# Eight-batch cross attention and non-local block: the first batch's keys and values in context chunks, the second half's rows kept whole, and new engine orders

## Time and profile before

| | us |
|---|---|
| median of 3 runs (lowest, highest) | 1065.98 (1063.28, 1066.46) |
| the profiled execution | 1065.61 |
| its span, first to last instruction | 1063.8 |
| TensorE busy in it | 1042.0 |
| VectorE busy | 722.1 |
| ScalarE busy | 480.6 |
| GpSimd busy | 280.5 |

### The profile page before, as it was taken

How to read it: one execution, slowest core, us unless ns; L and a number is a source line. 1 busy time by engine, 2 the same in 40 slices (tenths; PEclk the granted TensorE clock), 3 DMA queues, 4 the chain that set the end, 5 groups by cost and what they waited for, 6 DMA issues and landing times.

```text
span 1063.8 us, 13869 instructions
## 1 busy us (share of the span) xinstructions
PE 1042.0 (98%) x5104; PEld 850.5 (80%) x5104; DVE 722.1 (68%) x961; ACT 480.6 (45%) x810; POOL 280.5 (26%) x199
## 2 busy tenths in 40 slices
...
DMA packets 80627, 122.06 MB, mean 115 GB/s; under 512 B 13104, under 2 KB 46384, under 8 KB 80560
## 3 DMA queue, kind: packets, MB, share of 16 engines
...
## 4 chain that ended last, share of the span: by engine, by line
PE 88%; DVE 6%; DMA 3%; ACT 1%; issue 1%; SPq 0%; DVEq 0%; ACTq 0%
PE pG L573 33%; PE pG L472 13%; PE pG L584 8%; PE pG L480 6%; PE pG L513 4%; PE pG L487 4%; PE pT L594 3%; PE pS L525 3%; PE pT L525 2%; PE pG L594 2%; PE pM L552 2%; PE pM L561 2%; PE pS L451 2%; PE pT L462 2%; DVE xr L902 2%; DMA out_dram<-xr 1%
## 5 line engine op out<-in xcount | busy, mean ns | idle before, releaser
L573 PE MATMUL pG<-pt,vT 128*128 128x512 f32 x1536 | 352.9, 389 | 1.0 <-DVE pt L852 1.0
L573 PEld LDWEIGHTS pG<-pt,vT 128*128 128x128 f32 x1536 | 287.2, 188 | 60.2 <-issue 1.2
L472 PE MATMUL pG<-wv,x2s 128*128 128x512 f32 x768 | 182.9, 393 | 0.5 <-DVE vT L799 0.4
L881 DVE SCALAR_TENSOR_TENSOR xr<-pG,cl,xr 128x512 f32<-128x512 f32 x64 | 48.0, 751 | 189.2 <-PE pG L573 179.9
L931 POOL TENSOR_TENSOR xms<-xr,xms 128x512 fp32r<-128x512 f32 x64 | 87.7, 1370 | 319.6 <-ACT xms L726 319.6
L472 PEld LDWEIGHTS pG<-wv,x2s 128*128 128x128 f32 x768 | 142.1, 188 | 33.3 <-issue 3.3
L726 ACT ACTIVATE xms<-xr 128x512 fp32r<-128x512 f32 x64 | 40.3, 629 | 203.9 <-DVE xr L881 203.9
L852 DVE TENSOR_TENSOR pt<-mv,pt 128x512 fp32r<-128x512 f32 x128 | 89.8, 753 | 35.6 <-ACT pt L703 35.6
L923 POOL TENSOR_TENSOR x2Ts<-x2T_f,x2Ts 128x512 fp32r<-128x512 f32 x64 | 90.5, 1452 | 72.8 <-ACT x2Ts L672 72.7
L927 POOL TENSOR_TENSOR ys<-yf,ys 128x256 fp32r<-128x256 f32 x32 | 27.3, 854 | 306.1 <-ACT ys L694 306.1
L584 PE MATMUL pG<-xms,wth 128*128 128x512 f32 x384 | 90.1, 391 | 0.0
...
## 6 DMA issues: line engine op xcount, KB each, us to landing
mv<-tp SPq DMA_DIRECT2D x512, 64.0 KB, 2.0
...
```

The costliest lines, as they stand in the source:

```text
L472: last = mm(bank, x2s[:, l, c, 128 * m:128 * m + 128], wv[:, r, c, :], start=(c == 0 and n == 0), stop=(c == 3 and n == 2))
L573: last = mm(bank, vT[:, l, m, 128 * c:128 * c + 128], pt(h)[:, r, m, :], start=(m == 0 and n == 0), stop=(m == 7 and n == 2))
```

## The change

Three things are edited, and the orders are written anew.

1. In batch 0, `k:0 k:1 v:0 v:1` and `v:2 v:3` become `kv:0` to `kv:3`: for each context chunk as it lands, its share of `k` and of four value tiles. They accumulate in six banks at once, `pS`, `pG` and `pM` (`v_bank`). The `wv` chunks are loaded between the context chunks.
2. In half 1, ScalarE adds the constant to the row buffer in place (`xc:c`, after the low part was made), `wy:1,c` adds the product to that and is stored from there; `out:1,c` is gone. In half 0, `wy` and `out` write to `oh`, in the place of the low part, and have a semaphore of their own for the stores (`s_so`), so that `wy:1,c` no longer waits for the store of half 0.
3. ScalarE's `x2T` waits for the last `th` product and no longer for `out:1,c`. Its `k` and `q` wait for stores of half 0.

The lists `FIRST` and `LATER` change for TensorE, ScalarE and VectorE, the same words otherwise, and in particular `x2:2`, `x2:3`, `xs:1` and `x1:1` of the next batch go behind `th:1,1` on ScalarE, and `gs` behind `v:2` on TensorE. GpSimd's lists stay.

```diff
 FIRST = dict(
     pe=(
-        "k:0 k:1 v:0 v:1 q:0 q:1 v:2 v:3 S:0 S:1 v:4 S:2 L:0 L:1 L:2 S:3 L:3 gs S:4 G:0 G:1 gt G:2 G:3 v:5 S:5 "
...
+        "kv:0 kv:1 kv:2 kv:3 q:0 q:1 v:4 S:0 S:1 L:0 L:1 L:2 S:2 S:3 gs L:3 G:0 S:4 gt G:1 G:2 GT:0 G:3 GT:1 v:5 "
+        "S:5 S:6 v:6 v:7 Y:0 S:7 Y:1 Y:2 Y:3 PV:0,0,0 M:0 M:1 PV:0,0,1 PV:0,1,0 PV:0,1,1 PV:0,2,0 B:0 B:1 "
...
     act=(
...
+        "w:0 x2:0 w:1 w:2 x2:1 xs:0 x2:2 w:3 xs:1 x2:3 w:4 xs:2 x1:0 w:5 x1:1 xs:3 x1:2 x1:3 k s v:0 k2 x2T:0 q "
+        "v:1 x2T:1 v:2 x2T:2 x2T:3 q2 x2T:4 v:3 v:4 x2T:5 x2T:6 x2T:7 w:6 S:0 L:0 w:7 S:1 L:1 L:2 gs S:2 L:3 S:3 "
+        "gt G:0 G:1 S:4 T:0 G:2 GT:0 G:3 w:8 GT:1 T:1 v:5 v:6 S:5 v:7 T:2 Y:0 T:3 Y:1 Y:2 Y:3 S:6 S:7 mts T:4 "
...
 LATER = dict(
     pe=(
-        "gs k:0 k:1 q:0 q:1 v:0 v:1 v:2 S:0 S:1 gt L:0 L:1 S:2 L:2 S:3 L:3 G:0 S:4 G:1 GT:0 G:2 G:3 v:3 S:5 v:4 "
-        "v:5 v:6 GT:1 v:7 Y:0 S:6 S:7 Y:1 Y:2 Y:3 PV:0,0,0 M:0 M:1 PV:0,0,1 PV:0,1,0 PV:0,1,1 B:0 B:1 PV:0,2,0 "
+        "k:0 k:1 q:0 q:1 v:0 v:1 v:2 gs S:0 S:1 L:0 L:1 L:2 gt S:2 S:3 L:3 G:0 G:1 G:2 GT:0 GT:1 G:3 S:4 S:5 v:3 "
+        "v:4 v:5 v:6 v:7 Y:0 S:6 S:7 Y:1 Y:2 Y:3 PV:0,0,0 M:0 M:1 PV:0,0,1 PV:0,1,0 B:0 B:1 PV:0,2,0 PV:0,1,1 "
...
     act=(
-        "xs:2 xs:3 s x1:2 x1:3 k x2T:0 x2T:1 x2T:2 q x2T:3 x2T:4 x2T:5 v:0 x2T:6 q2 v:1 k2 x2T:7 gs v:2 gt S:0 "
-        "L:0 L:1 S:1 L:2 S:2 L:3 S:3 G:0 GT:0 G:1 T:0 S:4 v:3 T:1 G:2 G:3 v:4 v:5 T:2 GT:1 v:6 S:5 v:7 T:3 Y:0 "
-        "Y:1 Y:2 Y:3 S:6 S:7 mts PV:0,0 PV:0,1 T:4 T:5 T:6 B:0 B:1 T:7 PV:0,2 PV:0,3 PV:1,0 PV:1,1 PV:1,2 +x2:0 "
-        "PV:1,3 +x2:1 th:0,0 +xs:0 +x2:2 th:0,1 +x1:0 +x2:3 th:1,0 +x1:1 +xs:1 th:1,1"
+        "x2:2 xs:1 x2:3 xs:2 x1:1 x1:2 x1:3 xs:3 x2T:0 x2T:1 x2T:2 q s k x2T:3 v:0 x2T:4 x2T:5 q2 x2T:6 k2 v:1 "
+        "v:2 gs x2T:7 S:0 L:0 S:1 gt L:1 L:2 S:2 L:3 S:3 G:0 GT:0 T:0 G:1 G:2 v:3 GT:1 G:3 S:4 T:1 v:4 v:5 S:5 "
+        "v:6 T:2 v:7 Y:0 T:3 Y:1 Y:2 Y:3 S:6 mts S:7 PV:0,0 T:4 T:5 T:6 PV:0,1 PV:0,2 T:7 PV:0,3 PV:1,0 PV:1,1 "
+        "B:0 PV:1,2 xc:0 B:1 +x2:0 xc:1 xc:2 th:0,0 PV:1,3 +x2:1 xc:3 th:0,1 +x1:0 th:1,0 +xs:0 th:1,1"
     ),
     dve=(
-        "k q v:0 q2 k2 v:1 v:2 S:0 S:1 n:0 tr:0 S:2 n:1 tr:1 S:3 n:2 tr:2 G:0 S:4 G:1 n:3 G:2 tr:3 G:3 T:0 G2:0 "
-        "G2:1 v:3 T:1 G2:2 G2:3 GT:0 v:4 S:5 v:5 n:4 tr:4 GT:1 v:6 n:5 v:7 Y:0 tr:5 T:2 Y:1 T:3 Y:2 Y:3 S:6 S:7 "
-        "n:6 tr:6 mt n:7 mts tr:7 PV:0,0 PV:0,1 T:4 T:5 T:6 PV:0,2 B:0 T:7 B:1 PV:0,3 PV:1,0 PV:1,1 PV:1,2 PV:1,3 "
-        "+x2:0 +x2:1 th:0,0 +x2:2 th:0,1 +x2:3 th:1,0 th:1,1 wy:0,0 wy:0,1 out:0,0 wy:0,2 +s wy:0,3 out:0,1 "
-        "wy:1,0 out:0,2 out:0,3 wy:1,1 out:1,0 out:1,1 wy:1,2 wy:1,3 out:1,2 out:1,3"
+        "s q v:0 k q2 k2 v:1 v:2 S:0 S:1 n:0 tr:0 n:1 S:2 tr:1 S:3 n:2 G:0 tr:2 G:1 G:2 n:3 G2:0 tr:3 G:3 S:4 "
+        "GT:0 S:5 T:0 v:3 G2:1 n:4 G2:2 GT:1 v:4 tr:4 v:5 T:1 G2:3 n:5 v:6 v:7 T:2 Y:0 tr:5 Y:1 T:3 Y:2 S:6 Y:3 "
+        "n:6 tr:6 S:7 mt mts n:7 PV:0,0 tr:7 T:4 PV:0,1 T:5 PV:0,2 T:6 T:7 PV:0,3 PV:1,0 PV:1,1 PV:1,2 B:0 PV:1,3 "
+        "B:1 +x2:0 th:0,0 +x2:1 th:0,1 th:1,0 th:1,1 +x2:2 wy:0,0 out:0 wy:0,1 +x2:3 out:1 wy:0,2 wy:0,3 out:2 "
+        "out:3 wy:1,0 wy:1,1 wy:1,2 wy:1,3"
     ),
...
+        oh = [at(f"oh{c}", [128, 512], F, rd + 4096 * c + 2048) for c in range(4)]
...
+        def v_bank(b, m):
+            if b == 0 and m in (2, 3):
+                return pM[:, m - 2, :]
+            return bank_of(use_v(b, m))
...
+                        dst = out[b, 128 * c:128 * c + 128, 512 * h:512 * h + 512]
+                        if h:
+                            wait_free(eng, b, G_WY + 4 + c)
+                            eng.dma_start(dst, xr[c][:, :]).then_inc(s_st[c], 16)
+                        else:
+                            wait(eng, "oa", b, c)
+                            eng.dma_start(dst, oh[c][:, :]).then_inc(s_so[c], 16)
...
+            def do_kv(b, c):
+                if c == 0:
+                    eng.wait_ge(s_wlo, W_K + 1)
+
+                def k_mm(part):
+                    for h in range(2):
+                        last = mm(pS[:, h, :], wk[:, c, :], x2s[:, part, c, 512 * h:512 * h + 512],
+                                  start=(c == 0 and part == HI), stop=(c == 3 and part == LO))
+                        if c == 3 and part == LO:
+                            done(last, "k")
+
+                def v_mm(m, n):
+                    l, r = PASSES[n]
+                    return mm(v_bank(0, m), x2s[:, l, c, 128 * m:128 * m + 128], wv[:, r, c, :],
+                              start=(c == 0 and n == 0), stop=(c == 3 and n == 1))
+
+                wait(eng, "x2hi", 0, c)
+                k_mm(HI)
+                eng.wait_ge(s_whi, W_V + 1 + c)
+                if c < 3:
+                    for m in range(4):
+                        v_mm(m, 0)
+                    wait(eng, "x2lo", 0, c)
+                    k_mm(LO)
+                    for m in range(4):
+                        v_mm(m, 2)
+                    eng.wait_ge(s_wlo, W_V + 1 + c)
+                    for m in range(4):
+                        v_mm(m, 1)
+                else:
+                    wait(eng, "x2lo", 0, c)
+                    k_mm(LO)
+                    eng.wait_ge(s_wlo, W_V + 1 + c)
+                    for m in range(4):
+                        v_mm(m, 0)
+                        v_mm(m, 2)
+                        done(v_mm(m, 1), "g")
+
...
             def do_x2T(b, m):
                 eng.wait_ge(s_x2Td[m // 2], 16 * (b + 1))
                 if b:
-                    wait(eng, "oa", b - 1, 4 + m // 2)
+                    wait(eng, "g", b - 1, G_TH + 3)
...
+            def do_xc(b, c):
+                wait(eng, "xlo", b, 4 + c)
+                if b == 0:
+                    eng.wait_ge(s_cst, 4)
+                done(act(xr[c][:, :], xr[c][:, :], ACT.Identity, bias=cst(c)), "xc")
...
             def do_wy(b, h, c):
                 i = G_WY + 4 * h + c
                 wait(eng, "g", b, i)
-                if h == 0:
-                    wait(eng, "xlo", b, 4 + c)
+                if h:
+                    wait(eng, "xc", b, c)
+                    done(stt(out=xr[c][:, :], in0=bank_of(i), scalar=gain(c), in1=xr[c][:, :],
+                             op0=ALU.mult, op1=ALU.add), "gf")
                 else:
-                    eng.wait_ge(s_st[c], 16 * (2 * b + 1))
-                done(stt(out=xr[c][:, :], in0=bank_of(i), scalar=gain(c), in1=xms(h)[:, c, LO, :].bitcast(F),
-                         op0=ALU.mult, op1=ALU.add), "gf")
-
-            def do_out(b, h, c):
-                wait_free(eng, b, G_WY + 4 * h + c)
-                done(stt(out=xr[c][:, :], in0=xr[c][:, :], scalar=cst(c), in1=xms(h)[:, c, HI, :].bitcast(F),
+                    done(stt(out=oh[c][:, :], in0=bank_of(i), scalar=gain(c), in1=xms0[:, c, LO, :].bitcast(F),
+                             op0=ALU.mult, op1=ALU.add), "gf")
+
+            def do_out(b, c):
+                wait_free(eng, b, G_WY + c)
+                done(stt(out=oh[c][:, :], in0=oh[c][:, :], scalar=cst(c), in1=xms0[:, c, HI, :].bitcast(F),
                          op0=ALU.add, op1=ALU.add), "oa")
```

More of the change, by code:

```diff
@@ L25 @@
     t1k=1, t1q=1, khi=1, qhi=1, vhi=8, exp=8, Thi=8, Ghi=4, Lhi=4, GThi=2, Yhi=4, shi=1, s_rowc=1, s_colc=1, mthi=1, Bhi=2,
-    xhi=8, thhi=4, x2hi=4, x1hi=4, x2Thi=8,
+    xhi=8, xc=4, thhi=4, x2hi=4, x1hi=4, x2Thi=8,
     kf=4, qf=2, klo=1, qlo=1, gf=36, mx=8, rec=8, norm=8, tr=8, Tlo=8, Glo=4, GTlo=2, slo=1, gsum=2, mtf=2, mtlo=1, Blo=2,
-    x2sum=4, x2lo=4, oa=8,
+    x2sum=4, x2lo=4, oa=4,
     x2Tlo=8, Ylo=4, xlo=8, x1lo=4,
@@ L236, in xattn_kernel @@
         s_st = [sem(f"s_st{i}") for i in range(4)]
+        s_so = [sem(f"s_so{i}") for i in range(4)]
         s_mv = [sem(f"s_mv{i}") for i in range(8)]
```

32 lines of the change are left out of this document (16 added, 16 removed), and 22 rows, old and new, of tables (act, dve, pe).

## The result

The changed kernel takes 1086.0 us (1084.17 to 1086.45, 4 runs) against 1065.94 for the kernel before: a ratio of 1.019, with a 95% interval from 1.017 to 1.0211. It is slower by 20 us, as forecast. The profiled execution took 1086.45 us and its span is 1084.7 us, 20.9 above the 1063.8 of before.

What follows compares the result with a forecast made beforehand. It took TensorE's in-order matmul stream (busy 1042.0 of 1063.8 us) as the bound. Seam +26.0, matmul stream -3.5, start +0.5 and end -2.1 gave +20.9 on 1065.6: 1086 us, forecast case 1080 to 1093, whole range 1061 to 1093.

Steps and rivals of the forecast that it cites:

- The seam decides: Between batches, first `th` to `S:0`: late ScalarE splits make GpSimd's x1 parts and VectorE's `out` collide; +26.0 us.
- Z: Time zero of a seam: the start of the first theta matmul (`th:0,0`) of a batch.
- the four seams that I took at 4.1: Seams other than those in batches 2 to 4: `S:0` at Z+42.6 against 38.5, 4.1 us later each.
- the three at 3.2: Seams in batches 2 to 4, where the old seam was already 1.4 to 2.7 late: 3.2 us each.
- the 0 to 5 that the bound gave: Lower bound of the seam term: with no mutual holding of VectorE and GpSimd, 0 to 5 us in all.
- The engine that waited gets the turn: VectorE and GpSimd in the seam: GpSimd, having waited 0.4 us, goes next, 17.25 to 19.65, with `out:1` behind it.
- an order by who starts first: Seam, the skill's port lock: by that alone VectorE could keep the port for its next operation, the 20 us case.
- The matmul stream: Later batches: four `S` groups instead of six, 0.25 us each (bounds 0.1 and 0.3): -0.5 a batch, -3.5 for seven.
- `T:1`, now far back on VectorE: Later batches: `T:3` ready 0.9 us before `PV:0,0,0`, so no cost; without that cover up to 1 us a batch.
- The start: Batch 0: `kv` ends at 24, `S:0` at 34.8, first exponential some 3 us later; +0.5 us, from -3 to +2.
- in effect 0.4 us lost: Batch 0, up to `S:0`: at 34.8 instead of 31.70, with `v:4` (2.7 us) already done.
- The end: After the last matmul: one `wy` instead of two `wy` and two `out`; -2.1 us.

Runs made afterwards that it cites:

- e1: The changed kernel with `x2:2`, `x2:3`, `xs:1`, `x1:1` ahead of `th:1,1` again on ScalarE, `xc` fitted in around them: 1058.62 us, ratio 0.9942.
- e2: The changed kernel without `out` in half 0 (its output lacks the constant and high part there): 1070.43 us, ratio 1.0057.
- e10: The changed kernel with x1's low parts made on VectorE and none on GpSimd, late ScalarE words kept: 1069.12 us, ratio 1.0035.
- e4: The kernel before with parts 2 and 3 of the change alone; orders, loads and batch 0 as before: 1062.57 us, ratio 0.9978.
- e5: Batch 0 of e4 with the later-batch order of e1: 1055.32 us, ratio 0.9901.
- e11: e9 with `T:1` earlier on VectorE in later batches, right behind `v:4`: 1054.2 us, ratio 0.9895.
- e12: e5 with `T:1` earlier on VectorE in later batches, right behind `v:4`: 1054.73 us, ratio 0.9899.
- e9: e8 with the `q` chain and all `x2T` also ahead of the first exponential in batch 0, VectorE's words to match: 1054.96 us, ratio 0.9909.
- e8: e1 with `PV:0,0` and `PV:0,1` ahead of `T:4` on ScalarE in batch 0, `tr:7` earlier on VectorE: 1057.1 us, ratio 0.9928.
- e3: The changed kernel with `out:1` moved behind `wy:0,2` and `wy:0,3` on VectorE: 1085.84 us, ratio 1.0202.

## Why the prediction was right, step by step

**The seam decides: right, in mechanism, place and nearly in size.** Forecast against measured, from Z: `th:1,1` on ScalarE 11.17, 10.9; GpSimd's first x1 part of three 16.8, 16.6; `out:1` done 20.3, 19.9; stall in front of `wy:1,2` 1.7, 1.5; `out:3` done 26.4, 25.5; `x2T` loads 26.75, 25.9; from there to the third tile 6.2, 6.2; `S:0` 42.6, 41.9. All but the landing of the third tile are 0.2 to 0.9 early or short, most of it in `out:2` and `out:3`. The term was mis-sized by that: 26.0 forecast, 22.2 measured (14.9 for the four seams that I took at 4.1, 7.3 for the three at 3.2). e1 shows that the ScalarE order is its cause, e2 and e10 that about 17 of the 22 are VectorE and GpSimd holding each other, and that what is left without it is 5.2, just over the 0 to 5 that the bound gave. Up to 1.6 of the 22.2 are neither: in the seam into batch 4 TensorE's granted clock was 0.50 from 569 to 571 us, and `v:2` and `gs` took 1.6 us longer; the forecast does not have that.

**The engine that waited gets the turn: right.** `x2:3` on VectorE ended at 944.44, with GpSimd's part asking since 943.99 and `out:1` next on VectorE. Had VectorE kept its turn, `out:1` would have ended near 945.2; it ended at 947.24, so the 2.40 us of GpSimd's part went first. And the three parts took 8.30 us and not 7.2, since VectorE's operations got their turns between them: GpSimd's second part began at 946.64, while `out:1` had stood since 944.36, and `out:1` was done 0.55 after the first part. The Trainium skill, SBUF — State Buffer, section "SBUF: two separate sides", has the lock, and e10 agrees: with no GpSimd operation beside it `out` took 759 ns at most. The prediction took an order by who starts first to leave VectorE free to keep its turn. In the records GpSimd's part starts first (943.99, `out:1` 944.36), so the rows fit such an order as well, if the start of a record that still waits counts. That the waiting engine is served next is only in the rows.

**The matmul stream: right in the sum, wrong in both parts.** Fewer `S` groups gave not 0.5 but 0.8 us a batch (`S:0` to the first PV 41.61 to 41.66 before, 40.79 to 40.82 after, in batches without a wait), so 5.7 in all, 0.4 for each group and above the bound of 0.3. e4 has the old order and 41.6, e5 the new one and 40.8, so it is the order; that it is the number of groups alone was not tested. And "`T:1`, now far back on VectorE" did cost: the first PV waits for `T:3` or `Y` in three batches (up to 1.3 us), and second halves for 0.1 to 1.0. Against stretches without a wait that is 4.1 us in all; I had 0.9 us of cover and took nothing. The kernel before lost 1.5 in these stretches, and not by a wait: in batch 2, after a wait of 2.33 us for `klo`, TensorE ran at a granted clock of 0.50 from 295.5 to 298.5. Without that the term would have been -1.6 and not -3.1, so its hit is luck. e11 and e12, with `T:1` moved forward, have none of the first kind.

**The start: the failed step is "in effect 0.4 us lost".** `kv` ended at 23.89 (24 forecast), and full pace came at 12.06, not at the 16.4 of the kernel before. The Trainium skill, TensorE: Matmul & The Clock Gate, section "What's actually happening", has activity release the clock; by that alone I had 23.4, and the trace agrees within 0.5. But `S:0` came at 36.08, not 34.8: I had counted ScalarE's copies alone, and `klo` and `qlo` on VectorE lie beside GpSimd's x2T parts (L983), which held `qlo` up by 1.1:

```profile
33.66 2.28 DVE L854 TENSOR_TENSOR qlo<-qf,qhi 128x1024 fp32r<-128x1024 f32 x1
```

In e4, where it began between two of GpSimd's parts, the same `qlo` took 1.22. The first exponential came 6.1 us later than before, not 3, and the first PV 1.5 later (75.98 against 74.5). What sets that first PV stays open: e9, e11 and e12 have `S:0` 1.3 to 3.4 earlier than the changed kernel and the first PV only 0.3 to 0.6. The other 2.4 us I had not looked for: `PV:0,0` behind `T:4` on ScalarE, which puts GpSimd among VectorE's `T` parts. e8 shows this one by itself.

**The end: right**, 2.0 of 2.1.

**An error that was nearly free.** `v:2` waits for a bank in all seven seams (8.8 us in all), which the forecast does not have. In five seams it is in the shadow of `klo`: `S:0` waited 3.4 us for that besides. Into batch 4 it was not: the wait of 1.78 us was followed by the slow stretch named above. e3 shows how such waits trade places while the end stays.

So +3.4 at the start and -3.8 at the seam cancelled in the sum. That the kernel is slower, by the seam, is the mechanism; that the time is 1086.0 and the forecast 1086 is luck.
